# Graph attention: a pipeline two blocks deep, and one-hot matrices made on ScalarE

## What is computed

```python
ft = (feat @ W).reshape(n, H, D)
a1 = jnp.einsum('nhd,hd->nh', ft, attn_l)
a2 = jnp.einsum('nhd,hd->nh', ft, attn_r)
e = jax.nn.leaky_relu(a1[src] + a2[dst], negative_slope=ALPHA)
m = jax.ops.segment_max(e, dst, num_segments=n)
ex = jnp.exp(e - m[dst])
s = jax.ops.segment_sum(ex, dst, num_segments=n)
alpha = ex / s[dst]
out = jax.ops.segment_sum(ft[src] * alpha[:, :, None], dst, num_segments=n)
```

## Time and profile before

| | us |
|---|---|
| median of three runs | 10816.34 |
| lowest and highest | 10788.65, 10819.21 |
| the profiled execution | 10808.19 |
| its span | 10806.5 |
| first and last L1542 (one per block of the attention) start at | 7036.0, 9614.3 |

### The profile page before, as it was taken

One profiled execution on the slowest core, in us unless ns is written; L12 is line 12 of the kernel. 1 busy time (PEld: TensorE's weight loads), 2 busy tenths in 40 slices (PEclk: granted clock), 3 DMA queues, 4 the chain that ended last, 5 costly groups with the idle time before them and its releaser, 6 DMA issues. The chain is left out here.

```text
span 10806.5 us, 124673 instructions
## 1 busy us (share of the span) xinstructions
PE 6733.9 (62%) x23840; PEld 4708.7 (44%) x23841; DVE 5013.1 (46%) x16052; ACT 1610.9 (15%) x3209; POOL 5030.3 (47%) x5307
## 2 busy tenths in 40 slices
PE   5565555555554444444579998566666666640999
PEld 3453343433443333333345555444444444420666
DVE  6834444444333333333321211177777777786111
ACT  0010000000000000000122221222222222222222
POOL 0027777777657777777300000066666666630000
PEclk6555555555555555555557776666667666765999
DMA  1101111111100000000000001144444444421000
GB/s 40 48 21 26 26 26 26 26 26 26 22 16 13 13 13 13 13 13 13 6 6 0 0 0 63 55 123 116 120 117 120 117 116 120 118 82 34 16 16 16
DMA packets 352968, 481.08 MB, mean 45 GB/s; under 512 B 147816, under 2 KB 253262, under 8 KB 352750
## 3 DMA queue, kind: packets, MB, share of 16 engines
q0 software_dynamic: 198016, 334.70, 12.6%
q1 hardware_dynamic: 154734, 144.44, 4.1%
HBM read 429.61 MB, written 49.16 MB: 44 GB/s over the span
## 5 line engine op out<-in xcount | busy, mean ns | idle before, releaser
L554 POOL DMA_INDIRECT conv_rows<-table,conv_idx x3520 | 3345.8, 951 | 1852.2 <-issue 1072.0
L628 PE MATMUL conv_pm<-conv_rows,conv_sel 128*128 128x64 f32 (+1 forms) x7040 | 2284.2, 423 | 2175.6 <-DMA conv_rows<-table,conv_idx 2175.6
L628 PEld LDWEIGHTS conv_pm<-conv_rows,conv_sel 128*128 128x128 f32 x7040 | 1763.4, 311 | 2696.3 <-DMA conv_rows<-table,conv_idx 1386.5
L1288 POOL DMA_INDIRECT att_rows<-ft_rows,att_idx x1760 | 1667.6, 948 | 2658.7 <-ACT att_idx L1302 2161.3
L616 DVE TENSOR_TENSOR acc<-acc,conv_pm 128x64 f32 (+1 forms) x3520 | 719.6, 204 | 2303.5 <-PE conv_pm L628 1521.9
L1433 PE MATMUL att_pm<-att_rows,att_sel 128*128 128x264 f32 x3520 | 1403.0, 563 | 171.1 <-DVE sums L1581 159.3
L600 DVE TENSOR_SCALAR conv_sel<-iota,edges,edge_w 128x128 f32<-128x128 f32 x3528 | 994.5, 367 | 444.4 <-issue 413.2
L1433 PEld LDWEIGHTS att_pm<-att_rows,att_sel 128*128 128x128 f32 x3520 | 910.7, 278 | 484.2 <-DVE sums L1581 245.4
L1581 DVE TENSOR_TENSOR sums<-sums,att_pm 128x264 f32 x1760 | 753.1, 428 | 347.9 <-PE att_pm L1433 150.2
L544 ACT ACTIVATE conv_idx<-edges 128x8 int32 x440 | 91.4, 208 | 4304.5 <-PE conv_pm L628 4253.2
L1551 DVE TENSOR_TENSOR att_rows<-att_rows,att_pwi 128x1056 f32<-128x1056 f32 x440 | 547.6, 1245 | 134.0 <-issue 86.2
(11 more groups left out here) (304 smaller groups left out, 6725.3 us busy)
## 6 DMA issues: line engine op xcount, KB each, us to landing
conv_rows<-table,conv_idx POOLq DMA_INDIRECT x3520, 2.3
att_bc<-places SPq DMA_DIRECT2D x110, 512.0 KB
att_rows<-ft_rows,att_idx POOLq DMA_INDIRECT x1760, 3.1
ft_rows<-proj_ft SPq DMA_DIRECT2D x25, 544.0 KB, 3.0
x_spilled<-x_rows SPq DMA_DIRECT2D x1, 12800.0 KB, 39.7
elu_xg<-x_spilled SPq DMA_DIRECT2D x25, 512.0 KB
x_rows<-x SPq DMA_DIRECT2D x6, 2048.0 KB, 18.7
out<-ffn_y SPq DMA_DIRECT2D x24, 512.0 KB, 2.9
```

Source lines behind the costliest of these rows:

```text
L554: pool.indirect_dma_start(out=dest(k), out_offset=None, in_=table, in_offset=bass.IndirectOffsetOnAxis(ap=idx[:, k:k + 1], axis=0)).then_i ...
L628: ins = nc.tensor.matmul(pm[q % RING][:, i, :], sel[:, (q % RING) * QUAD + i, :], rows[:, k, :], start=True, stop=True)
L1288: pool.indirect_dma_start(out=rows[:, k, :], out_offset=None, in_=K.ftd, in_offset=bass.IndirectOffsetOnAxis(ap=idx[:, k:k + 1], axis=0)). ...
```

## The change

Three things are changed, all in `attention`.

1. The chain of maxima runs two blocks ahead. In body b the block m = b + 2 goes from `attention_of` to `crossing` (the copy of the carries, taken out of `whole`), and n = b + 1 goes through `whole`, `exponents`, `weights` and all four `weigh`, so that the weights of a block are finished a block before its sums. A new semaphore `c_kept` holds `factor` back until the carries have been copied out of the PSUM tile that both use.
2. `hots` moves from VectorE to ScalarE: for each step |edge's place - column| over 128 columns with the place as a per-partition bias, and then one relu(1 - x) over the quad's 512 columns: five instructions in the place of one. The constant `count` in PSUM goes.
3. The order within each body is new, on all engines. The first half of `columns` is a function of its own, `distances`; it waits for `a_done`.

```diff
+            def hots(n, q):
+                s, at = n * SEGS + q * QUAD, q * QUAD
+                for k in range(QUAD):
+                    ins = act.activation(sel[:, at + k, :], K.iota[:, :], ACT.Abs, bias=K.edges[:, 1, ds(s + k, 1)],
+                                         scale=-1.0)
+                ins.then_inc(off, 1)
+                act.wait_ge(off, n * NQ + q + 1)
+                act.activation(sel[:, at:at + QUAD, :], sel[:, at:at + QUAD, :], ACT.Relu, bias=K.ones[:, 0:1],
+                               scale=-1.0).then_inc(sel_ready, 1)
...
-                if more:
-                    attention_of(*following(turn, i))
-                refill(0)
-                if more:
-                    ends(n)
-                    carries(n)
-                    weights(n)
-                refill(1)
-                if more and (not isinstance(b, int) or b + 2 < NB):
-                    columns(b + 2, (i + 2) % PERIOD)
+                if more:
+                    weights(n)
+                if most:
+                    act.wait_ge(a_done, n + 1)
+                    distances(m)
+                refill(0)
+                if more:
+                    hots(n, 0)
+                    hots(n, 1)
+                if most:
+                    columns(m, (i + 2) % PERIOD)
+                    attention_of(*following(turn, i, 2))
+                    ends(m)
+                refill(1)
+                if more:
+                    hots(n, 2)
+                if most:
+                    carries(m)
+                if more:
+                    hots(n, 3)
...
+                sums(b, i, 0, 0, 2)
                 if more:
+                    pe.wait_ge(c_kept, b + 2)
                 factor(b)
+                if more:
                     maxima_turned(n)
+                sums(b, i, 0, 2, QUAD)
...
+                if more:
+                    whole(n)
                 where = places(b, 0)
                 rescale(b, i, where)
-                add(b, 0, where)
-                weigh(b, i, 2)
+                add(b, 0, where, 0, 2)
+                if more:
+                    exponents(n)
+                add(b, 0, where, 2, QUAD)
+                if more:
+                    weigh(n, ni, 0)
...
                 where = places(b, 3)
+                add(b, 3, where)
+                if more:
+                    weigh(n, ni, 3)
+                if most:
+                    joined(m)
+                    crossing(m)
```

More of the change, by code:

```diff
@@ L1229, in attention @@
          x_turned, fl_loaded, th_loaded, local_done, row_done, row_kept, row_scanned, carry_kept, col_done, m_ready,
-         m_turned, d_ready, p_ready, f_done, chain, passed, set_up, split, counted, a2_kept) = (
+         m_turned, d_ready, p_ready, f_done, chain, passed, set_up, split, off, c_kept, a2_kept) = (
             ph.sem(x) for x in (
@@ L1233, in attention @@
                 "x_turned fl_loaded th_loaded local_done row_done row_kept row_scanned carry_kept col_done m_ready "
-                "m_turned d_ready p_ready f_done chain passed set_up split counted a2_kept").split())
+                "m_turned d_ready p_ready f_done chain passed set_up split off c_kept a2_kept").split())
         block = ph.block()
@@ L1312, in attention_of, with distances, columns @@
                 ins.then_inc(a1_ready, 1)
-            def columns(n, i):
+            def distances(n):
                 act.wait_ge(bc_loaded, n * 16 + 16)
                 act.activation(sel_t[:, :, :], bc[:, :, :], ACT.Abs, bias=K.ncol[:, 0:1]).then_inc(apart, 1)
+            def columns(n, i):
                 act.wait_ge(apart, n + 1)
@@ L1353, in _, with body @@
             weights(0)
+            for q in range(NQ):
+                hots(0, q)
+            act.wait_ge(a_done, 1)
+            distances(1)
             columns(1, 1)
-            def body(turn, i, more):
+            attention_of(0, 1)
+            ends(1)
+            carries(1)
+            def body(turn, i, more, most):
                 b = block_of(turn, i)
-                n = b + 1
+                n, m = b + 1, b + 2
                 def refill(k):
@@ L1519, in joined, with crossing, whole @@
                 dve.sem_inc(a2_kept, 1)
-            def whole(n):
+            def crossing(n):
                 dve.wait_ge(col_done, n + 1)
                 own.then(dve.tensor_copy(cc[:, :], pc))
+                dve.sem_inc(c_kept, 1)
+            def whole(n):
                 own.then(scan(my[:, :], fl[:, 0:P], mx[:, :], cc[:, 0:1], ALU.add, ALU.max))
@@ L1581, in add @@
                     tt(at[k], at[k], pm[k][:, 0:WIDTH], ALU.add).then_inc(added, 1)
-            PER = 1 + 3 + 1 + 2 + 6 + 1
+            AHEAD = 1 + 3 + 1 + 1
+            PER = AHEAD + 1 + 6 + 1
             own.did(dve.memset(K.acc[:, :, :, :], 0.0))
-            first = own.k
-            for q in range(NQ):
-                hots(0, q)
             local(0)
@@ L1590, in _, with body @@
             joined(0)
+            crossing(0)
             whole(0)
             exponents(0)
-            weigh(0, 0, 0)
-            assert own.k - first == PER - 1
+            for q in range(NQ):
+                weigh(0, 0, q)
+            local(1)
+            along(1)
+            joined(1)
+            crossing(1)
             start = own.start()
-            def body(turn, i, more):
+            def body(turn, i, more, most):
                 b = block_of(turn, i)
-                n, ni = b + 1, (i + 1) % PERIOD
+                n, m, ni = b + 1, b + 2, (i + 1) % PERIOD
                 own.turn(start, b, PER)
-                weigh(b, i, 1)
+                if not more:
+                    own.base -= AHEAD
+                if more:
+                    whole(n)
                 where = places(b, 0)
                 rescale(b, i, where)
-                add(b, 0, where)
-                weigh(b, i, 2)
+                add(b, 0, where, 0, 2)
                 if more:
-                    hots(n, 0)
+                    exponents(n)
+                add(b, 0, where, 2, QUAD)
+                if more:
+                    weigh(n, ni, 0)
                 where = places(b, 1)
@@ L1610, in body @@
                 if more:
-                    local(n)
-                weigh(b, i, 3)
-                if more:
-                    hots(n, 1)
-                    along(n)
-                    joined(n)
+                    weigh(n, ni, 1)
                 where = places(b, 2)
                 add(b, 2, where)
+                if most:
+                    local(m)
                 if more:
-                    hots(n, 2)
-                    whole(n)
+                    weigh(n, ni, 2)
+                if most:
+                    along(m)
                 where = places(b, 3)
-                add(b, 3, where, 0, 2)
+                add(b, 3, where)
                 if more:
-                    exponents(n)
-                    weigh(n, ni, 0)
-                add(b, 3, where, 2, QUAD)
-                if more:
-                    hots(n, 3)
+                    weigh(n, ni, 3)
+                if most:
+                    joined(m)
+                    crossing(m)
                     assert own.k == PER
```

77 lines of the change are left out of this document (39 added, 38 removed).

## The result

| kernel | median of its runs, us | profiled run, us | span, us | mean granted clock |
|---|---|---|---|---|
| before, on the same chip | 10817.77 (10788.65 to 10820.85) | 10808.19 | 10806.5 | 0.613 |
| changed | 11065.78 (11053.48 to 11083.6) | 11083.6 | 11081.9 | 0.606 |

The ratio is 1.024, with a 95% interval of 1.0217 to 1.0263. The forecast was 10920, the range 10720 to 11045: the kernel is slower, as forecast, but by 248 us where 112 were forecast, and the time lies 21 us above the range, within the times of the rival "longer than I say". The profiled execution of the changed kernel is the slowest of its four, 18 us above the median; the traces therefore have 275 us to explain.

The account below looks back on a forecast made before the run. VectorE's work and the chain through it bound a block; after the change, the chain through ScalarE. A block of 24.6 us against 23.65 gives 105 us, the end 7, the start 0: 10808 + 112 = 10920 us, range 10720 to 11045.

Parts of the forecast that it names:

- longer than I say: Rival: low clock throughout and `hots` at 2.3 us a quad, block 25.5 us, 11000 to 11105 us; chance 12%.
- Where ScalarE's new work stands: ScalarE, behind the first index copy: two quads of one-hots, 3.8 us, ahead of the logit copies; logits ready at R + 6.45.
- The low clock in the fourth quad: TensorE idles 3 to 4 us before the turning, so the fourth quad probably starts at the low clock; worth 1.25 us.
- from `whole` to the next R: From the scan opening `whole` to ScalarE's next first index copy: 7.2 us, or 8.2 by the second quad's low-clock sums.
- The sum of small steps to `whole`: From the first index copy through logits, turning, `local`, `along`, additions and `weigh` to the next `whole`: R + 16.5 us.
- The branch: At the end of each three-block loop turn: stays at 2.5 us a turn, all on the path.
- The tail: After the last exponents: a block and a half of additions where before one; +7 us.
- The start of the attention itself: `hots` four times and a second chain of maxima, about 18 us, replace an equally long first block's: 0.
- GpSimd as the bound: Rival: VectorE is relieved and GpSimd's gathers bound the block at 20.0 us plus 0.8 for the branch, 10505 us; chance 5%.
- The shorter chain: Rival: fourth quad at the high clock, `hots` at 1.4 us a quad, or both; 10775 us, both 10670; chance 18%.
- The longer chain: Rival: low clock throughout and one-hots at 2.3 us a quad, period 24.7 + 0.8 us, up to 11105 us; chance 12%.
- The cancelling rival: Rival: gain and loss cancel, with a period of 22.6 to 23.1 us, 10776 to 10840 us; chance 12%.

Follow-up runs that it names:

- l1: Changed kernel with the four absolute differences of each of the first two quads left out from block 1 on; 10648.28 us, ratio 0.9859.
- e4: Changed kernel with TensorE's register loads of block numbers for all later quads gathered behind the third quad's sums, before the turning; 11019.56 us, ratio 1.0194.
- e5: Changed kernel with ScalarE's logit copies moved ahead of the one-hots, directly behind the first index copy; 10634.49 us, ratio 0.9839.
- e2: Kernel before, with its one stage, and only the one-hots moved to ScalarE, in gaps of its stream; 10608.51 us, ratio 0.9822.
- e6: Changed kernel with six blocks in a loop turn in place of three; 11005.59 us, ratio 1.0194.
- c2: e2 with six blocks in a loop turn in place of three; 10544.74 us, ratio 0.9758.
- c3: Kernel before with six blocks in a loop turn in place of three; 10744.41 us, ratio 0.9948.
- c1: e5 with e4's gathered register loads and six blocks in a loop turn; 10955.55 us, ratio 1.014.
- f1: e5 with TensorE's register loads gathered ahead of the turning, three blocks a turn, on a slower chip; 12796.21 us, ratio 0.9921.

## Why the prediction was right in kind and too small

**Where ScalarE's new work stands.** Right, and the signs named for it are there: VectorE idle before the first scan with the turning as releaser, TensorE idle before the turning, ended by the logit copy. They are larger than named, 3.5 and 4.3 us. Times of the one block shown above, from R, the first index copy (8015.01):

| step | measured | forecast |
|---|---|---|
| two quads of `hots` | 3.86 | 3.8 |
| logits copied | R + 6.53 | 6.45 |
| first scan of `local` | R + 7.09 | 7.05 |
| `along` | R + 10.68 | 10.6 |
| additions of the fourth quad | R + 13.05 | 12.8 |
| `whole` | R + 16.97 | 16.5 |
| last step of the exponents ready | `whole` + 5.07 | 4.8 |
| next R | `whole` + 8.2 | 7.3, from 7.2 to 8.2 |
| period inside a turn (median) | 25.17 | 23.8 |
| branch, per turn (median) | 3.0 | 2.45 |

**The low clock in the fourth quad.** Right: two sums take 2.12 us behind TensorE's 4.4 us of standing, and l1 shows the other level. In stretches of 2 us of the profile the granted clock is 1.00 when TensorE stops (8016 to 8018), 0.82 in the next and 0.50 from 8020 on: it fell while TensorE stood.

**The step that failed: from `whole` to the next R.** The working gave 7.2 to 8.2, the upper end being what TensorE's second quad needs behind two register loads at the low clock. I took 7.3, as if ScalarE's own stream set it. Measured is the upper end, 8.2. ScalarE's `distances` do end at `whole` + 7.4, but then ScalarE is idle for 0.85 us before the index copy, released by the sums (L1467). TensorE stands 0.90 before the second quad's sums, where two of the register loads are:

```profile
8010.97 6.24 PE L1467 MATMUL att_pm<-att_rows,att_sel 128*128 128x264 f32 x16 [0.90 <-DVE sums L1617]
```

It names VectorE's additions as the releaser; in e4, where the loads are gone from that place, the stretch falls to 7.26, which is ScalarE's own time. The low clock is the other condition that the working had set for its upper end, and it held: the granted clock is 0.50 in every such stretch from 8004 to 8014, while the first quad's sums and nearly all of the second's run. In e4 the high clock comes back sooner. Both stretches below, the changed kernel's and then e4's, begin 4.0 us behind a `whole`, in blocks without a branch:

```profile
8036.00:8038.00 2.00, 1.85 (x4) 1.50 (x5) 1.90 (x8) 0.96 (x3) 1.18 (x2) 0.50 0.37 115
```

```profile
8014.00:8016.00 2.00, 1.38 (x6) 0.69 (x6) 1.90 (x8) 0.96 (x3) 1.19 (x2) 0.95 0.38 113
```

How much of the 0.95 us is the loads alone and how much the clock is not parted. The term is worth 0.9 x 109 = 98 us of the 157 that the periods are above the forecast.

**The sum of small steps to `whole`.** Mis-sized by 0.47 us, 51 us over all: 0.08 up to `along`, 0.17 from there over the register load to the additions, 0.22 from the additions to `whole`.

**The branch.** Mis-sized: 3.0 us a turn, 0.18 us a block, 20 us. It cost 3.0 in the kernel before as well. The forecast's 2.5 came from the mean period over all 109, which the last blocks without a branch lower, and from one block of 22.82 us taken for both of its neighbours; the idle time of 2.49 in the earlier trace rows seemed to confirm it. In the changed kernel the idle time behind the branch stands in front of `whole`: `[3.34 <-issue]`. 98 + 51 + 20 = 169; a turn's mean is 26.17 us a block, and the last blocks, without a branch and shorter, bring it to the 26.06 of all 109: 12 us less, which gives the 157.

**The tail.** Right: +5.8, forecast +7. The start of the attention itself: 0.7, forecast 0. The 6.5 us in stages ahead of the attention were in no term.

**The rivals.** GpSimd as the bound did not come: it waits longer than before. The shorter chain is what e5 shows, but only in another order. The longer chain is what happened, at a chance of 12%, but in part by luck: that rival had the low clock throughout, which came for the first two quads and the first half of the fourth, and one-hots at 2.3 us a quad, which came out at 2.0 as laid out; the register loads, the branch and the small steps filled their place. The upper end of the failed step alone would have stayed in the range (10920 + 98 = 11018). With the small steps and the branch, all three to the same side, it did not. (The cancelling rival's lower bound is off by 14 us: a period of 22.6 gives 10790 by the prediction's own terms, not 10776. Nothing hangs on it.)

## What to carry to other kernels

An engine with free time is not free at every place: before work is moved to an idle engine, find what in its in-order stream others wait for, and put the new work behind that (here 431 us between two orders of the same instructions). Taking the same work out in two places, once ahead of and once behind the suspected instruction, tells in two runs whether it is the place or the amount. When two ends of a term differ by which engine sets it, price both, take the later one when its conditions are met elsewhere in the same layout (here the low clock), and let the range reach the worse ends together.

## What the runs showed of the chip that was not expected

- A turn of the hardware loop makes its block 3.0 us longer in the kernel before and the changed one, 3.6 in e2, and 18 turns fewer gain 60 to 64 us (e6, c2, c3).
- Four register loads with the unpacking of four numbers each hold TensorE's stream 4.5 us (c1, f1), two of them leave 0.90 of idle time in the changed kernel. The profile shows it as idle time, put down to "issue" or to a semaphore that had already come.
- TensorE kept the clock of 2.4 GHz through 1.64 us of standing (l1) and came back at 1.2 GHz after 4.4 (the changed kernel) and 4.5 (c1).
- Chips differ: the kernel before took 10796 to 10818 us on the first ones used and 12890 to 13049 on the last three. On these three the variants of e5, whose order was 1.6% faster than the kernel before on another chip, are within 1% of it.
